# LSTM decoder stage: the output row selected in turned form, the sums of the exponentials on VectorE, and the normalising factor in the selecting columns

## The reference

```
gates   = x_t @ W_x + attn @ W_attn + hid @ W_hid + biases      # i, f, g, o; 256 each
cell    = sigmoid(f) * cell + sigmoid(i) * tanh(g)
hid     = sigmoid(o) * tanh(cell)
alpha   = softmax(hid @ Wq' @ context^T)                        # over 512 source positions
attn    = tanh(alpha @ context @ Wout_c + hid @ Wout_h + b_out) # also the step's output
```

## Time and profile before

| what | value |
|---|---|
| median of the runs | 6038.66 us |
| profiled execution, span from first to last instruction | 6037.1 us |
| recurrent stage, 258 to 4226 us | 3968 us |
| TensorE, VectorE, ScalarE busy over the whole span | 90%, 60%, 35% |
| TensorE, VectorE, ScalarE busy in the stage | 3743, 2145, 1623 us |
| granted clock of TensorE, whole span and stage | 0.966, 1.00 |

### The profile page before, as it was taken

How to read it: one execution, slowest core, us unless ns; L and a number is a source line. 1 busy time by engine, 2 the same in 40 slices (tenths; PEclk the granted TensorE clock), 3 DMA queues, 4 the chain that set the end, 5 groups by cost and what they waited for, 6 DMA issues and landing times. The chain is left out here.

```text
span 6037.1 us, 384310 instructions
## 1 busy us (share of the span) xinstructions
PE 5442.3 (90%) x171160; PEld 3792.5 (63%) x171160; DVE 3651.2 (60%) x16434; ACT 2098.9 (35%) x7989; POOL 353.7 (6%) x811
## 2 busy tenths in 40 slices
PE   6899999999999999999999999999788888787989
PEld 2577777777777777777777777777544344334433
DVE  4355555555555555555555555555488999999931
ACT  3144444444444444444444444444222122223221
POOL 0000000000000000000000000000011211112000
PEclk8999999999999999999999999999888889898989
DMA  1100000000000000000000000000221111111111
GB/s 69 58 2 2 2 2 2 2 2 2 2 2 2 2 2 2 2 2 2 2 2 2 2 2 2 2 2 2 84 62 40 45 31 40 38 42 36 47 39 54
DMA packets 45131, 111.57 MB, mean 18 GB/s; under 512 B 8160, under 2 KB 10208, under 8 KB 44528
## 3 DMA queue, kind: packets, MB, share of 16 engines
q1 hardware_dynamic: 43600, 109.39, 5.9%
q10 hardware_dynamic: 1440, 1.06, 0.1%
HBM read 99.90 MB, written 10.52 MB: 18 GB/s over the span
## 5 line engine op out<-in xcount | busy, mean ns | idle before, releaser
L711 PE MATMUL lstm_part_ps<-lstm_keys,lstm_hid 128*4 128x128 f32 x32768 | 1025.2, 273 | 206.2 <-DVE lstm_hid L880 206.2
L727 PE MATMUL lstm_ctx_ps<-lstm_values,lstm_alpha 128*4 128x128 f32 (+1 forms) x49152 | 1052.0, 237 | 0.2 <-issue 0.2
L711 PEld LDWEIGHTS lstm_part_ps<-lstm_keys,lstm_hid 128*4 128x4 f32 x32768 | 770.7, 86 | 429.8 <-DVE lstm_hid L880 415.7
L727 PEld LDWEIGHTS lstm_ctx_ps<-lstm_values,lstm_alpha 128*4 128x4 f32 x49152 | 901.4, 86 | 94.5 <-issue 0.4
L909 DVE TENSOR_REDUCE lstm_neg_max<-lstm_part_ps 128x1 f32<-128x128 f32 x1024 | 298.6, 292 | 679.5 <-PE lstm_part_ps L711 679.5
L842 ACT ACTIVATE lstm_expo<-lstm_part_ps,lstm_neg_max 128x128 f32<-128x128 f32 x1024 | 375.9, 367 | 863.5 <-DVE lstm_neg_max L909 863.5
L670 PE MATMUL lstm_half_ps<-lstm_w_hid,lstm_hid 128*13 128x96 f32 x16384 | 595.8, 246 | 0.0
L862 DVE STREAM_TRANSPOSE lstm_gates<-lstm_half_ps 128x96 f32<-128x96 f32 x1026 | 290.2, 283 | 397.3 <-PE lstm_half_ps L670 373.2
L670 PE MATMUL lstm_half_ps<-lstm_w_attn,lstm_attn 128*13 128x96 f32 x16448 | 525.8, 248 | 0.0
L670 PEld LDWEIGHTS lstm_half_ps<-lstm_w_attn,lstm_attn 128*13 128x13 f32 x16448 | 300.1, 93 | 155.7 <-ACT lstm_attn L855 107.0
L1945 ACT ACTIVATE mix_gated<-mix_gate_ps 115x512 f32<-115x512 f32 (+2 forms) x200 | 112.6, 563 | 778.5 <-PE mix_gate_ps L1673 778.4
(11 more groups left out here) (325 smaller groups left out, 8500.5 us busy)
## 6 DMA issues: line engine op xcount, KB each, us to landing
mix_ring<-in_sm_chunks SPq DMA_DIRECT2D x120, 358.0 KB, 2.9
mix_ring<-in_mix_chunks SPq DMA_DIRECT2D x80, 384.0 KB, 3.0
lstm_xg<-xg_rows SPq DMA_DIRECT2D x514, 16.0 KB
xg_rows<-lstm_xg_tile SPq DMA_DIRECT2D x16, 512.0 KB, 2.6
ctxT<-in_ctxT SPq DMA_DIRECT2D x1, 2048.0 KB, 14.6
out_xT<-xT SPq DMA_DIRECT2D x4, 512.0 KB, 3.8
xT<-in_xT SPq DMA_DIRECT2D x1, 1536.0 KB, 9.7
lstm_w_x<-in_lstm_w_x SPq DMA_DIRECT2D x1, 1024.0 KB, 10.0
```

Source lines behind the costliest of these rows:

```text
L711: mm = pe.matmul(part_rows(score_ps[part], b), hid[:, k, lo:lo + SPACE], keys[:, k, b * SRC + c * P:b * SRC + (c + 1) * P], start=(n == 0 ...
L727: mm = pe.matmul(part_rows(ctx_ps[n], b), alpha[:, b, c, SPACE - 1 - c:2 * SPACE - 1 - c], values[:, b * SC + c, ctx_cols[n]], start=(c == ...
```

## The change

- The exponentials give no accumulator output any more. VectorE sums each half by a TENSOR_REDUCE of expo (sum_part), the first after L915, the second behind the copy of the second turned rows; the spread of the totals waits for both.
- The first turned rows are copied into alpha by ScalarE, between the two exponentials; alpha_ready becomes two semaphores.
- factor goes. In its place VectorE makes sel_shrunk (sel_batch times own shrink, four columns) and sel_scaled (sel_shrunk times the inverse, plus hidden_sel, which has the hid rows' ones). The three pieces of the output row are plain copies.
- select(o) has 32 columns of out_row as the stationary operand and sel_scaled as the moving one, with a wait for sel_ready ahead of select(0). The result has features on partitions. The tanh of ScalarE reads it from PSUM; attn_in and its two transpositions go.

```diff
@@ masks @@
-SEL, OWN_PART, HIDDEN_ROWS, PLACE = 0, BATCH, BATCH + SC, BATCH + SC + 1
+SEL, OWN_PART, HIDDEN_SEL, PLACE = 0, BATCH, BATCH + SC, 2 * BATCH + SC
...
-        hidden_rows = masks[:, HIDDEN_ROWS:HIDDEN_ROWS + 1]
+        hidden_sel = masks[:, HIDDEN_SEL:HIDDEN_SEL + BATCH]
...
-            factor = q.sb("lstm_factor", [P, 1])
+            sel_shrunk = q.sb("lstm_sel_shrunk", [P, BATCH])
+            sel_scaled = q.sb("lstm_sel_scaled", [P, BATCH])
             out_row = q.sb("lstm_out_row", [P, DIM])
-            attn_in = q.sb("lstm_attn_in", [P, KC, STRIP])
...
-            attn_ps = [part_ps[o][:, P:P + STRIP] for o in range(KC)]
+            attn_ps = [part_ps[o][:, P:P + BATCH] for o in range(KC)]
...
+            def alpha_rows(part):
+                return alpha[:, :, 2 * part:2 * part + 2, SPACE - 1]
+
+            def turned_rows(part):
+                return turned_ps[part].rearrange("p (b r) -> p b r", r=2)
 
             @block.sync
             def _(sp):
...
 
                     for j in range(QUARTERS):
                         lo = o * P + j * STRIP
-                        mm = pe.matmul(attn_ps[o][j * STRIP:j * STRIP + BATCH, :], sel_batch, out_row[:, lo:lo + STRIP],
+                        mm = pe.matmul(attn_ps[o][j * STRIP:(j + 1) * STRIP, :], out_row[:, lo:lo + STRIP], sel_scaled[:, :],
                                        start=True, stop=True)
                     mm.then_inc(attn_summed[o], 1)
 
...
                         turn(0)
                         hidden_part()
                         half_hid(0, 0)
-                        pe.wait_ge(alpha_ready, 2 * t + 1)
+                        pe.wait_ge(alpha_ready[0], t + 1)
                         for n in range(PIECES):
                             context(0, n)
                         pe.wait_ge(exp_ready, 2 * t + 2)
                         turn(1)
                         for n in range(PIECES):
                             context(1, n)
-                        pe.wait_ge(alpha_ready, 2 * t + 2)
+                        pe.wait_ge(alpha_ready[1], t + 1)
                         for n in range(PIECES):
                             context(2, n)
                             context(3, n).then_inc(ctx_ready[n], 1)
                         half_hid(1, 0)
+                        pe.wait_ge(sel_ready, t + 1)
                         pe.wait_ge(out_row_ready[0], t + 1)
                         select(0)
                         half_hid(0, 1)
...
                             act.activation(tanh_c[:, k, :], cell[:, k, GATES - 1, :], ACT.Tanh, scale=0.5).then_inc(c_tanh[k], 1)
                         for part in range(PARTS):
                             act.wait_ge(max_ready, 2 * t + part + 1)
-                            act.activation(expo[:, part, :], score_ps[part], ACT.Exp, bias=neg_max[:, part:part + 1],
-                                           accum_out=total[:, part:part + 1]).then_inc(exp_ready, 1)
+                            act.activation(expo[:, part, :], score_ps[part], ACT.Exp, bias=neg_max[:, part:part + 1])\
+                               .then_inc(exp_ready, 1)
+                            if part == 0:
+                                act.wait_ge(alpha_turned, 2 * t + 1)
+                                act.copy(alpha_rows(0), turned_rows(0)).then_inc(alpha_ready[0], 1)
                         act.wait_ge(max_all_ready, t + 1)
                         act.activation(by_part(shrink[:, :]), spread_values(spread_max[:, :]), ACT.Exp, scale=-1.0,
                                        bias=neg_max_all[:, :]).then_inc(shrink_ready, 1)
                         act.wait_ge(ctx_ready[0], t + 1)
-                        act.wait_ge(factor_ready, t + 1)
-                        act.mul(out_row[:, 0:P], ctx_ps[0], factor[:, 0:1]).then_inc(out_row_ready[0], 1)
+                        act.copy(out_row[:, 0:P], ctx_ps[0]).then_inc(out_row_ready[0], 1)
                         act.wait_ge(ctx_ready[1], t + 1)
-                        act.mul(out_row[:, ctx_cols[1]], ctx_ps[1], factor[:, 0:1]).then_inc(out_row_ready[1], 1)
+                        act.copy(out_row[:, ctx_cols[1]], ctx_ps[1]).then_inc(out_row_ready[1], 1)
                         act.wait_ge(attn_kept, t + 1)
                         for o in range(KC):
-                            act.wait_ge(attn_turned[o], t + 1)
-                            act.activation(by_batch(attn[:, o, :]), attn_in[:, o, 0:BATCH], ACT.Tanh).then_inc(attn_ready[o], 1)
+                            act.wait_ge(attn_summed[o], t + 1)
+                            act.activation(by_batch(attn[:, o, :]), attn_ps[o], ACT.Tanh).then_inc(attn_ready[o], 1)
 
             @block.vector
             def _(dve):
...
                     dve.scalar_tensor_tensor(out=by_batch(hid[:, k, PAD:]), in0=by_batch(o_col[:, k, :]), scalar=1.0,
                                              in1=tanh_c[:, k, :], op0=ALU.add, op1=ALU.mult).then_inc(h_ready[k], 1)
 
-                def keep_turned(t, part):
-                    dve.wait_ge(alpha_turned, 2 * t + part + 1)
-                    turned = turned_ps[part].rearrange("p (b r) -> p b r", r=2)
-                    dve.tensor_copy(alpha[:, :, 2 * part:2 * part + 2, SPACE - 1], turned).then_inc(alpha_ready, 1)
+                def sum_part(t, part):
+
+                    dve.wait_ge(exp_ready, 2 * t + part + 1)
+                    dve.tensor_reduce(total[:, part:part + 1], expo[:, part, :], AX_X, ALU.add).then_inc(total_part_ready, 1)
 
                 for ps in (*half_ps, *part_ps, *ctx_bank):
                     dve.memset(ps[:, :], 0.0)
...
                             dve.wait_ge(scores_ready, 2 * t + part + 1)
                             dve.tensor_reduce(neg_max[:, part:part + 1], score_ps[part], AX_X, ALU.max, negate=True)\
                                .then_inc(max_ready, 1)
-                        keep_turned(t, 0)
                         dve.wait_ge(max_ready, 2 * t + 2)
                         dve.transpose(spread_blocks(spread_max[:, :]), every_row(neg_max[:, :])).then_inc(max_spread, 1)
                         dve.wait_ge(max_spread, t + 1)
                         dve.tensor_reduce(neg_max_all[:, :], spread_values(spread_max[:, :]), AX_XY, ALU.min)\
                            .then_inc(max_all_ready, 1)
-                        dve.wait_ge(exp_ready, 2 * t + 2)
+                        sum_part(t, 0)
+                        dve.wait_ge(alpha_turned, 2 * t + 2)
+                        dve.tensor_copy(alpha_rows(1), turned_rows(1)).then_inc(alpha_ready[1], 1)
+                        sum_part(t, 1)
+                        dve.wait_ge(total_part_ready, 2 * t + 2)
                         dve.transpose(spread_blocks(spread_total[:, :]), every_row(total[:, :])).then_inc(total_spread, 1)
-                        keep_turned(t, 1)
                         dve.wait_ge(shrink_ready, t + 1)
                         dve.wait_ge(total_spread, t + 1)
                         dve.scalar_tensor_tensor(out=by_part(weighed[:, :]), in0=by_part(shrink[:, :]), scalar=1.0,
                                                  in1=spread_values(spread_total[:, :]), op0=ALU.mult, op1=ALU.mult,
                                                  accum_out=total_sum[:, :]).then_inc(total_ready, 1)
                         dve.scalar_tensor_tensor(out=own_terms[:, :], in0=shrink[:, :], scalar=1.0, in1=own_part,
-                                                 op0=ALU.mult, op1=ALU.mult, accum_out=own_shrink[:, :])
+                                                 op0=ALU.mult, op1=ALU.mult, accum_out=own_shrink[:, :]).then_inc(own_ready, 1)
                         dve.wait_ge(total_ready, t + 1)
                         dve.reciprocal(inverse[:, :], total_sum[:, :]).then_inc(inverse_ready, 1)
+                        dve.wait_ge(own_ready, t + 1)
+                        dve.tensor_scalar(sel_shrunk[:, :], sel_batch, own_shrink[:, 0:1], None, ALU.mult).then_inc(sel_shrunk_ready, 1)
                         dve.wait_ge(inverse_ready, t + 1)
-                        dve.tensor_scalar(factor[:, :], own_shrink[:, :], inverse[:, 0:1], hidden_rows, ALU.mult, ALU.add)\
-                           .then_inc(factor_ready, 1)
+                        dve.wait_ge(sel_shrunk_ready, t + 1)
+                        dve.scalar_tensor_tensor(out=sel_scaled[:, :], in0=sel_shrunk[:, :], scalar=inverse[:, 0:1],
+                                                 in1=hidden_sel, op0=ALU.mult, op1=ALU.add).then_inc(sel_ready, 1)
                         dve.wait_ge(ctx_ready[2], t + 1)
-                        dve.wait_ge(factor_ready, t + 1)
-                        dve.tensor_scalar(out_row[:, ctx_cols[2]], ctx_ps[2], factor[:, 0:1], None, ALU.mult)\
-                           .then_inc(out_row_ready[1], 1)
-                        for o in range(KC):
-                            dve.wait_ge(attn_summed[o], t + 1)
```

(13 more changed lines are left out.)

## The result

The changed kernel takes 6020.67 us (8 runs, 6016.49 to 6022.11) against 6036.02 us of the kernel before beside it: a ratio of 0.9972, 95% interval 0.9962 to 0.9982. It is faster by 0.3%, 15 us instead of the 118 forecast; that is clear of no change, and outside the range. The profiled execution's span is 6020.3 us; one step takes 7.718 us instead of 7.751 (mean of the starts of 512 steps), 0.033 us and not 0.23.

What follows compares the result with a forecast made beforehand. The profile names TensorE, but the prediction looked to four stops of its stream in each recurrent step. Ending at 2012.15 instead of 2012.38 saves 0.23 us, times 512 is 118 us: span 5919, median 5921; range 5865 to 5985.

Steps and rivals of the forecast that it cites:

- Parts 1 and 2: Exponentials without accumulator, first turned rows copied by ScalarE: context sums start 0.105 us earlier, bounds 0 and 0.15.
- rival B: First 0.105 us does not arrive because exponential 1 or turn(1) is held; 5975 us, chance 0.12.
- Part 3: Sums on VectorE, 0.29 us each: the first covered by idle time, the second and the spread new on the path.
- Part 4: Factor into the four columns on VectorE: selection 0 moves from 2011.17 to 2011.23, 0.06 us later.
- the forecast's own case: Measured time of the changed kernel lies at 5875 to 5965 us; chance 0.68.
- Part 5: Turned selection without transposition: the gates' second attention part starts at 2012.15 instead of 2012.38.
- A: VectorE's chain longer: full spacing (+0.09) and both pointer operations at 0.273 (+0.11); 6023 us, chance 0.06.
- C: Wide weight loads of the two selections do not overlap: step loses 0.12 us, 6100 us, chance 0.04.
- sign against the forecast: Forecast is wrong if the loads of L744 fill more than 0.2 us.
- D: VectorE's new operations cost like plain ones (0.16), selection 0 at 2011.11: gain 0.35 us, 5860 us, chance 0.08.
- E: ScalarE copy brings its own table load or the compiler keeps the read-out; some hundred us slower with loads, chance 0.02.

Runs made afterwards that it cites:

- e4: Changed kernel with its second sum ahead of the copy of the second turned rows instead of behind it; 5853.2 us.
- e1: Changed kernel with the two waits ahead of sel_scaled in the other order, sel_shrunk_ready first; 5977.5 us.
- e2: Changed kernel with both pairs of VectorE waits, ahead of sel_scaled and of weighed, in the other order; 5940.0 us.
- e5: Changed kernel with exponentials, copies and spread of the totals as before, leaving the turned selection and scaled columns alone; 5892.5 us.
- e10: e5 with TensorE's two waits ahead of selection 0 in the other order; 5858.9 us.
- e6: Kernel before with only the sums on VectorE and the first copy of turned rows on ScalarE; 6295.9 us.
- e11: e4 with one semaphore counted up twice in place of each pair of waits, ahead of weighed, sel_scaled and selection 0; 5813.2 us.

## Why the prediction was wrong, by its own steps

**Parts 1 and 2 held.** Turn(0) starts 0.091 earlier (1.486 instead of 1.577), the second copy at 2.789 (forecast 0.105 earlier, measured 0.094). Exponential 1 did not move (1.943 in both): rival B's hold did not happen. ScalarE's copy of 8 columns takes 0.173, inside the 0.16 to 0.18 forecast, but that range does not follow from the two rows named for it: 0.04 for 64 columns, taken from 0.223, leaves about 0.19.

**Part 3 held.** The sums take 0.276, not 0.29, and the copy ahead of them is 0.014 later than forecast; the two cancel, and the spread ends at 3.430, as its forecast of 2010.38 says (3.43 in the step). That the first sum was covered held as well. What part 3 missed is a choice: it took the order of sum and copy as given and did not ask whether the cover would hold the second sum too. e4 shows that this was worth 167 us.

**Part 4 failed.** Its line "an own result costs 0.036 (18.4 us of idle over 512 in front of L930)" was used for every operation of the chain. L930 has one wait. Weighed and sel_scaled have two, and the late one stands alone: 0.104 and 0.115. That is 0.07 + 0.08 = 0.15 of the 0.164 us by which selection 0's first load was later (4.444 against 4.28); nearly all the rest is the two pointer operations, 0.230 and 0.222 against 0.222 and 0.212. e1 and e2 show the 0.15: with both late waits carried the kernel takes 5940 us, which the forecast's own case (5875 to 5965) holds. The kernel before already had a pair in front of weighed, but its late wait was met long before, behind the copy; that the operation would lose this cover was the thing to see, since the text said that the spread had been done already. And the price itself stood in the trace of the kernel before, on another engine: the first tanh of attn_in has two waits in front of it, attn_kept and attn_turned[0], the late one second and so alone (L854), and starts 0.094 behind its transposition; the second tanh has one wait and starts 0.034 behind its own.

```profile
2011.48 0.22 DVE L938 STREAM_TRANSPOSE lstm_attn_in<-lstm_part_ps 128x32 f32<-128x32 f32 x1
...
2011.79 0.54 ACT L855 ACTIVATE lstm_attn<-lstm_attn_in 128x4 f32<-128x4 f32 x2 [0.47 <-DVE lstm_attn_in L938]
```

**Part 5 held within 0.04, with one reading wrong.** Selection 1's first matmul starts 0.411 behind selection 0's (forecast 0.39), the first load of the attention part's second quarter 0.545 behind that (forecast 0.53); tanh starts 0.096 behind the selection's modelled end, not 0.075, and takes 0.178. The idle time of 0.05 to 0.1 that was to vanish before selection 1 was none for the matmuls: they start 0.062 behind the last half_hid matmul in the kernel before as in the changed one, where the forecast took 0.04. The selection alone was worth 144 us (e5), with TensorE's pair of waits in order 176 us (6035.0 - 5858.9, e10).

**Rivals.** A gave the right time, 6023, for the wrong reason, so its nearness is luck: VectorE's chain was longer by 0.164 us, but neither by full spacing (copy to sum is 0.083 in the trace) nor by dear pointer operations (0.222 to 0.230). The section on the DRAIN that the prediction quotes from the Trainium skill, VectorE: DVE Perf Modes, goes on that a next op which is not held starts earlier; the 0.083 agrees with that sentence and not with the one quoted. Its chance of 0.06 was too small for another reason: I priced the known operations finely and gave no room to a price of the joints between them. C fell: the 32-column loads last 0.109, selection 0's eight fill 0.16 and selection 1's 0.21, and the matmuls behind selection 0 start 0.024 later than with four columns. The 0.21 is over the 0.2 that was named as a sign against the forecast, yet it costs nothing: the matmul in front of it is 0.062 away as before, and the last of the o gate's hid matmuls starts 0.356 behind selection 1 against 0.358 in the kernel before. The Trainium skill, TensorE: Matmul & The Clock Gate, section on LDWEIGHTS, has columns / 1.2 ns for a load; an estimate from it, eight of them in series, is 213 ns. Selection 0's row of 0.16 is under that although one load here shows as 0.109 and not 0.027, so the loads overlap. D did not happen, nor did E: the loop of the changed kernel holds no table load and no read-out of the accumulator on ScalarE.

## What to carry to other kernels

Where two waits stand in front of one instruction, find out which of them the builder lets the instruction carry (here the first in the source), and give it the late one, or count one semaphore up from both; on a path of 512 steps 0.08 us each is 41 us. Before work is moved onto an engine's chain, look where that engine is idle earlier in the step: here the same sum, one line earlier, was covered in full. When a fix makes another input the late one, the order has to be looked at again.

## What the runs showed of the hardware that was not expected

- A wait that is an instruction of its own and comes late costs 0.07 to 0.08 us more than one that the instruction carries on VectorE (0.104 and 0.115 against 0.035) and 0.09 on TensorE (0.146 against 0.055 to the first matmul, 0.115 against 0.053 to the first load). On ScalarE, where the order was not turned, the first tanh of the kernel before shows 0.094 against 0.034 for the second. Already met it cost under 0.01 us on VectorE. The Trainium skill, Perfetto Trace Analysis, section on sequencer-only instructions, has the sequencer itself wait and fetch the next instruction only afterwards; the prices are in line with that, though no run here looks inside the sequencer.
- The tanh that reads four columns from PSUM takes 0.178 us, the one from SBUF took 0.209; ScalarE's pass of 128 columns 0.265 as a plain copy, 0.367 with a pointer operand.
- Two independent reductions of 128x128 on VectorE fill 0.47 us, not 0.55: they overlap by 0.08, as the small operations do (0.17 long, 0.083 apart).
- The first matmul of selection 0 or 1 starts no less than 0.06 us behind the last half_hid matmul wherever no lone wait came late at selection 0, with weights of 4 columns (the kernel before, e6) and of 32 (the changed kernel, e1 to e4, e10, e11).
